# Splitting feed-forward weights into two parts once, ahead of the batch, instead of in every pass

## What is computed

```python
def _L0_ffn_ref(x, lut, gate_idx, up_idx, down_idx):      # INTER = 1376
    def _ghost_linear(x, idx, lut):
        w = lut[idx]
        return jnp.einsum('bsh,oh->bso', x, w)
    gate = _ghost_linear(x, gate_idx, lut)
    up = _ghost_linear(x, up_idx, lut)
    h = jax.nn.silu(gate) * up
    return _ghost_linear(h, down_idx, lut)
...
# the attention block: q, k, v, gates, an mLSTM mixer, h_out, then
x1 = x + h_out @ w_out
h2 = _rmsnorm(x1, norm2_w)
mlp = jax.nn.silu(h2 @ w_gate) * (h2 @ w_up) @ w_down     # FF = 2048
return x1 + mlp
...
xn = _layernorm(x, axis=-1)
x = x + _L0_attn_ref(xn, ...) + _L0_ffn_ref(xn, lut, gate_idx, up_idx, down_idx)
```

## Time and profile before

| | |
|---|---|
| median of three runs | 2799.28 us (2798.49 to 2799.92) |
| span of the profiled execution | 2801.1 us |
| look-up, from the first index load to the last predicated copy | 53 to 267 us |
| the eight passes | 267 to 2801 us |
| TensorE busy | 2441.7 us, 87% |
| VectorE, GpSimd, ScalarE busy | 1345.3, 1318.5, 1097.4 us |
| device memory read, written | 201.6 MB, 17.1 MB |
| mean granted clock of TensorE | 0.994 of full |

### The profile page before, as it was taken

One profiled execution on the slowest core, in us unless ns is written; L12 is line 12 of the kernel. 1 busy time (PEld: TensorE's weight loads), 2 busy tenths in 40 slices (PEclk: granted clock), 3 DMA queues, 4 the chain that ended last, 5 costly groups with the idle time before them and its releaser, 6 DMA issues.

```text
span 2801.1 us, 35857 instructions
## 1 busy us (share of the span) xinstructions
PE 2441.7 (87%) x11024; PEld 1970.5 (70%) x11024; DVE 1345.3 (48%) x2210; ACT 1097.4 (39%) x1847; POOL 1318.5 (47%) x887
## 2 busy tenths in 40 slices
...
GB/s 102 82 82 83 42 68 98 97 54 68 80 101 83 51 71 98 91 60 68 78 99 87 48 72 100 98 53 68 85 97 83 52 69 98 93 58 68 79 99 86
DMA packets 85664, 220.60 MB, mean 79 GB/s; under 512 B 9664, under 2 KB 9664, under 8 KB 85520
## 3 DMA queue, kind: packets, MB, share of 16 engines
...
## 4 chain that ended last, share of the span: by engine, by line
PE 42%; issue 23%; POOL 20%; DVE 8%; ACT 4%; ACTq 0%; DVEq 0%; DMA 0%; POOLq 0%; SPq 0%
PE acc L354 11%; PE gate_bank L354 10%; PE up_bank L354 10%; POOL gu_lo L1288 8%; PE bank_a L354 5%; PE bank_b L354 5%; POOL dn_lo L1293 5%; POOL hidden_lo L1298 3%; POOL MX L1313 2%; POOL vw L1328 1%; DVE hn L1088 1%; ACT acc L662 1%; DVE xn L1200 1%; DVE st L833 1%; POOL rh L1235 1%
## 5 line engine op out<-in xcount | busy, mean ns | idle before, releaser
L1298 POOL TENSOR_TENSOR hidden_lo<-hm,hidden_hi 128x512 fp32r<-128x512 f32 x216 | 279.6, 1294 | 672.4 <-ACT hidden_hi L634 672.4
L1288 POOL TENSOR_TENSOR gu_lo<-raw_gu,gu_hi 128x1024 fp32r<-128x1024 f32 x217 | 520.8, 2400 | 83.1 <-ACT gu_hi L609 83.1
L634 ACT ACTIVATE hidden_hi<-hm 128x512 fp32r<-128x512 f32 x216 | 136.3, 631 | 832.2 <-PE acc L354 813.8
L939 DVE SCALAR_TENSOR_TENSOR th<-th,gate_bank 128x512 f32<-128x512 f32 x216 | 147.7, 684 | 601.3 <-ACT th L629 601.3
L354 PE MATMUL acc<-dn_hi,hidden_hi 128*128 128x512 f32 x864 | 348.1, 403 | 10.7 <-POOL hidden_lo L1298 10.7
L354 PE MATMUL acc<-dn_hi,hidden_lo 128*128 128x512 f32 x864 | 340.8, 394 | 0.0
L354 PE MATMUL acc<-dn_lo,hidden_hi 128*128 128x512 f32 x864 | 340.6, 394 | 0.0
L1293 POOL TENSOR_TENSOR dn_lo<-raw_dn,dn_hi 128x512 fp32r<-128x512 f32 x216 | 292.3, 1353 | 63.1 <-ACT dn_hi L614 63.0
L945 DVE SCALAR_TENSOR_TENSOR hm<-th,up_bank 128x512 f32<-128x512 f32 x216 | 148.3, 687 | 251.2 <-PE up_bank L354 250.5
L629 ACT ACTIVATE th<-gate_bank 128x512 f32<-128x512 f32 x216 | 129.3, 598 | 301.9 <-PE gate_bank L354 301.9
L609 ACT ACTIVATE gu_hi<-raw_gu 128x1024 fp32r<-128x1024 f32 x217 | 226.8, 1045 | 12.5 <-DMA raw_gu<-ffn_weights 12.5
...
## 6 DMA issues: line engine op xcount, KB each, us to landing
raw_gu<-w_gu SPq DMA_DIRECT2D x128, 512.0 KB, 3.9
raw_gu<-ffn_weights SPq DMA_DIRECT2D x89, 512.0 KB, 3.7
raw_dn<-w_dn SPq DMA_DIRECT2D x128, 256.0 KB, 2.7
raw_dn<-ffn_weights SPq DMA_DIRECT2D x88, 256.0 KB, 2.7
xn<-x SPq DMA_DIRECT2D x9, 1024.0 KB, 8.4
qkT<-idx SPq DMA_DIRECT2D x34, 256.0 KB, 2.8
qkT<-x SPq DMA_DIRECT2D x8, 1024.0 KB, 5.9
result<-xn ACTq DMA_DIRECT2D x32, 256.0 KB, 2.3
```

Of the source, the lines that this page charges most:

```text
L634: act.activation(HH[0][:], hm[:], ACT.Copy).then_inc(act_hid.sem, 1)
L939: dve.scalar_tensor_tensor(th[:], th[:], 1.0, GB[:], ALU.add, ALU.mult).then_inc(vec_gate.sem, 1)
L1288: pool.tensor_tensor(WGU[1][:, slot, :], raw_gu[:, slot, :], WGU[0][:, slot, :].bitcast(f32), ALU.subtract)\
L1298: pool.tensor_tensor(HH[1][:], hm[:], HH[0][:].bitcast(f32), ALU.subtract).then_inc(pool_hid.sem, 1)
```

## The change

Device memory holds the two parts of all 27 tiles' weights, `gu_parts` and `dn_parts`, twice the bytes of the raw weights. All are written during the look-up. For the ghost chunks ScalarE casts the upper part (`upper`, between the evaluations of the chunk that follows), GpSimd subtracts, and GpSimd issues the store of both parts. For the 16 MLP tiles, which are spread over the look-up one behind every second chunk (`MLP_AFTER`), SyncE loads the raw weights, GpSimd makes both parts (`split_mlp`: two casts and two subtractions), and SyncE stores them and loads the next tile's. In the passes SyncE loads the parts into `WGU` and `WDN`, which TensorE reads (1024 KB and 512 KB a tile, two slots each); the casts and subtractions of weights on ScalarE and GpSimd are gone from there. The look-up's third chunk is built in `hr` in place of `raw_dn`.

```diff
-        ffn = nc.dram_tensor("ffn_weights", (NF, P, GU + D), f32, kind="Internal").ap()
+        gu_parts = nc.dram_tensor("gu_parts", (NT, P, 2 * GU), f32, kind="Internal").ap()
+        dn_parts = nc.dram_tensor("dn_parts", (NT, P, 2 * D), f32, kind="Internal").ap()
...
-        WGU = [sb(f"gu_{s}", [P, 2, GU], f32r) for s in ("hi", "lo")]
-        WDN = [sb(f"dn_{s}", [P, 2, D], f32r) for s in ("hi", "lo")]
+        WGU = sb("gu", [P, 2, 2, GU], f32r)
+        WDN = sb("dn", [P, 2, 2, D], f32r)
...
         BANKS = [None, A, B, GB, UB, ACC[0], ACC[1], ACC[2]]
-        wbuf = [th[:], hm[:], raw_dn[:]]
+        wbuf = [th[:], hm[:], hr[:, :, :].rearrange("p h n -> p (h n)")[:, 0:D]]
+        staged = [HT[c // 2][:, (c % 2) * 2:(c % 2) * 2 + 2, :] for c in range(3)]
+
+        def ghost_place(t, c):
+            whole, at = (gu_parts, c) if c < 2 else (dn_parts, 0)
+            return whole[t].rearrange("p (z n) -> p z n", z=2)[:, :, at * D:(at + 1) * D]
         fl = "p a b -> p (a b)"
         b0 = [qbd[:, :, :].rearrange(fl), hn[:, :, :].rearrange(fl), kn[:, 0:2, :].rearrange(fl)]
...
+        MLP_AFTER = {2 * m + 1: m for m in range(NM)}
...
-            def load_gu(at, k, slot, src):
-
-                sp.wait_ge(pool_wgu.sem, pool_wgu.of(at, k, "lo") - 2)
-                sp.dma_start(raw_gu[:, slot, :], src).then_inc(ld_gu[slot], 16)
-
-            def load_dn(at, k, src):
-                sp.wait_ge(pool_wdn.sem, pool_wdn.of(at, k, "lo") - 1)
-                sp.dma_start(raw_dn[:], src).then_inc(ld_dn, 16)
...
-            with sp.Fori(0, NF) as t:
-                for c in range(3):
-                    sp.wait_ge(look_vec, t * LOOK_V + (c * LOOK_C + LOOK_CREDIT + 3 - LOOK_V))
-                    sp.dma_start(ixb[c], idx[bass.ds(t, 1), :, c * D:(c + 1) * D].rearrange("a p n -> (a p) n"))\
-                        .then_inc(ld_idx[c], 16)
-
-            sp.wait_ge(look_vec, NF * LOOK_V + LOOK_CREDIT + 3 - LOOK_V)
-            sp.dma_start(ixb[0], idx[0, :, 0:D]).then_inc(ld_idx[0], 16)
+            def load_gu(at, k, slot, tile):
+
+                sp.wait_ge(pe_up.sem, pe_up.of(at, k, "done") - 2)
+                src = gu_parts[tile] if isinstance(tile, int) else gu_parts[bass.ds(tile, 1), :, :].rearrange("a p n -> (a p) n")
+                sp.dma_start(WGU[:, slot, :, :].rearrange("p z n -> p (z n)").bitcast(f32), src).then_inc(ld_gu[slot], 16)
+
+            def load_dn(at, k, slot, tile):
+                sp.wait_ge(pe_down.sem, pe_down.of(at, k, "done") - 2)
+                src = dn_parts[tile] if isinstance(tile, int) else dn_parts[bass.ds(tile, 1), :, :].rearrange("a p n -> (a p) n")
+                sp.dma_start(WDN[:, slot, :, :].rearrange("p z n -> p (z n)").bitcast(f32), src).then_inc(ld_dn[slot], 16)
+
+            def load_mlp(m):
+                if m >= 2:
+                    sp.wait_ge(mlp_lo, 2 * m - 3)
+                sp.dma_start(raw_gu[:, m % 2, :], w_gu[m]).then_inc(ld_mlp_gu[m % 2], 16)
+                if m >= 1:
+                    sp.wait_ge(mlp_lo, 2 * m)
+                sp.dma_start(raw_dn[:], w_dn[m]).then_inc(ld_mlp_dn, 16)
+
+            def store_mlp(m):
+                z = m % 2
+                sp.wait_ge(mlp_lo, 2 * m + 2)
+                sp.dma_start(gu_parts[NF + m], WGU[:, z, :, :].rearrange("p z n -> p (z n)").bitcast(f32)).then_inc(st_mlp[z], 16)
+                sp.dma_start(dn_parts[NF + m], WDN[:, z, :, :].rearrange("p z n -> p (z n)").bitcast(f32)).then_inc(st_mlp[z], 16)
+
+            load_mlp(0)
+            for n in range(3 * NF + 1):
+                t, c = n // 3, n % 3
+                if n >= 3:
+                    sp.wait_ge(look_vec, (t - 1) * LOOK_V + c * LOOK_C + LOOK_CREDIT + 3)
+                sp.dma_start(ixb[c], idx[t % NF, :, c * D:(c + 1) * D]).then_inc(ld_idx[c], 16)
+                if n in MLP_AFTER:
+                    m = MLP_AFTER[n]
+                    store_mlp(m)
+                    if m + 1 < NM:
+                        load_mlp(m + 1)
 
             for c in range(3):
                 sp.wait_ge(st_w[c], 16 * NF)
-            sp.wait_ge(st_zero, 16)
-            load_gu((0, 0), 0, 0, ffn[0, :, 0:GU])
+            sp.wait_ge(st_zero, 16 * 2)
+            for z in range(2):
...
                     at = (b, half)
                     for t in range(NF):
-                        nxt = ffn[t + 1, :, 0:GU] if t + 1 < NF else w_gu[0]
-                        load_gu(at, t + 1, (half * NT + t + 1) % 2, nxt)
-                        load_dn(at, t, ffn[t, :, GU:])
+                        load_gu(at, t + 1, (half * NT + t + 1) % 2, t + 1)
...
-                                    w_gu[bass.ds(i * 2 + (q + 1), 1), :, :].rearrange("a p n -> (a p) n"))
-                            load_dn(at, i * 2 + t, w_dn[bass.ds(i * 2 + q, 1), :, :].rearrange("a p n -> (a p) n"))
...
-                wait(pe, pool_wgu, at, t, "lo")
+            def parts(w, slot, n):
+                return w[:, slot, 0, n * P:(n + 1) * P], w[:, slot, 1, n * P:(n + 1) * P]
+
+            def gate(at, t, slot, act, n_loads):
+                pe.wait_ge(ld_gu[slot], n_loads)
...
+            def down(at, t, slot, n_loads, first=False, last=False):
+                pe.wait_ge(ld_dn[slot], n_loads)
                 wait(pe, pool_hid, at, t, "lo")
                 for i in range(NB):
-                    mm = split(ACC[i][:], [pair(HH, S_, toks(i))], [pair(WDN, S_, slot, S_)], first=first, last=last)
...
-
-            def w_gu(at, k, slot, n_loads):
-                act.wait_ge(ld_gu[slot], n_loads)
-                act.wait_ge(pe_up.sem, pe_up.of(at, k, "done") - 2)
-                act.activation(WGU[0][:, slot, :], raw_gu[:, slot, :], ACT.Copy).then_inc(act_wgu.sem, 1)
-
-            def w_dn(at, k, slot):
-                act.wait_ge(ld_dn, load_count_dn(at, k))
-                act.wait_ge(pe_down.sem, pe_down.of(at, k, "done") - 2)
-                act.activation(WDN[0][:, slot, :], raw_dn[:], ACT.Copy).then_inc(act_wdn.sem, 1)
...
-            def look_up(t, first=False):
+            def upper(t, c, first=False):
+
+                act.wait_ge(look_vec, t * LOOK_V + ((c + 1) * LOOK_C + LOOK_CREDIT))
+                if not first:
+                    act.wait_ge(st_w[c], t * 16)
+                act.activation(staged[c][:, 0, :], wbuf[c], ACT.Copy).then_inc(ghost_hi, 1)
...
                     act.wait_ge(look_vec, t * LOOK_V + ((c - 1) * LOOK_C + LOOK_CREDIT + 4))
                     if not first:
-                        act.wait_ge(st_w[c], t * 16)
+                        act.wait_ge(ghost_lo, (t - 1) * 3 + (c + 1))
                     for k in range(LUT // 2):
...
+                        if k == 3 and c:
+                            upper(t, c - 1, first)
+                        elif k == 3 and not first and not second:
+                            upper(t + -1, 2)
...
-            w_gu((0, 0), 0, 0, 16)
+            upper(NF - 1, 2)
+            act.wait_ge(st_zero, 16 * 2)
...
                             hid(at, t - 1)
-                        w_gu(at, t + 1, 1 - slot, gu_loads(at, t + 1))
                         tanh(at, t)
                         if t < UNITS:
...
+            def split_mlp(m):
+                z = m % 2
+                pool.wait_ge(ld_mlp_gu[z], 16 * (m // 2 + 1))
+                pool.wait_ge(st_mlp[z], 32 * (m // 2))
+                pool.tensor_copy(WGU[:, z, 0, :], raw_gu[:, z, :]).then_inc(mlp_hi, 1)
+                pool.wait_ge(ld_mlp_dn, 16 * (m + 1))
+                pool.tensor_copy(WDN[:, z, 0, :], raw_dn[:]).then_inc(mlp_hi, 1)
+                pool.wait_ge(mlp_hi, 2 * m + 2)
+                pool.tensor_tensor(WGU[:, z, 1, :], raw_gu[:, z, :], WGU[:, z, 0, :].bitcast(f32), ALU.subtract)\
+                    .then_inc(mlp_lo, 1)
+                pool.tensor_tensor(WDN[:, z, 1, :], raw_dn[:], WDN[:, z, 0, :].bitcast(f32), ALU.subtract)\
+                    .then_inc(mlp_lo, 1)
+
+            split_mlp(0)
+            for n in range(3 * NF):
+                t, c = n // 3, n % 3
+                pool.wait_ge(ghost_hi, n + 1)
+                pool.tensor_tensor(staged[c][:, 1, :], wbuf[c], staged[c][:, 0, :].bitcast(f32), ALU.subtract)\
+                    .then_inc(ghost_lo, 1)
+                pool.wait_ge(ghost_lo, n + 1)
+                pool.dma_start(ghost_place(t, c), staged[c].bitcast(f32)).then_inc(st_w[c], 16)
+                if n in MLP_AFTER and MLP_AFTER[n] + 1 < NM:
+                    split_mlp(MLP_AFTER[n] + 1)
             pool.wait_ge(vec_pre, 10)
             pool.wait_ge(st_w[2], 16 * NF)
             first = INTER - (NF - 1) * P
-            pool.dma_start(ffn[NF - 1, first:P, GU:], zero_rows[first:P, :]).then_inc(st_zero, 16)
-
-            def w_gu(at, k, slot):
-                wait(pool, act_wgu, at, k, "hi")
-                pool.tensor_tensor(WGU[1][:, slot, :], raw_gu[:, slot, :], WGU[0][:, slot, :].bitcast(f32), ALU.subtract)\
-                    .then_inc(pool_wgu.sem, 1)
...
```

(25 more changed lines are left out.)

74 lines of the change are left out of this document (26 added, 48 removed).

## The result

The changed kernel takes 2905.86 us (median of 4 runs, 2904.72 to 2906.16), the kernel before 2799.60 (4 runs, 2798.49 to 2800.13) on the same chip: 1.0381 times as long, 95% interval 1.0367 to 1.0396. The forecast was 2923, range 2855 to 3000. The profiled execution has a span of 2904.0 us, 102.9 more than before, and that splits in two: TensorE's first pass starts 174.3 us later (at 441.3 for 267.0), the passes are 73.3 us shorter together, and 1.9 are left at the program's end.

A forecast was written before the change was run, and what follows sets the result against it. TensorE was taken to bound the passes and VectorE's own chain the look-up. 2801.1 + 184 (look-up) - 2 (its end) - 58 (passes) = 2925, less 1.8 from span to median: 2923 us, range 2855 to 3000.

The forecast's parts named there:

- (d): Look-up: from the index's arrival to the end of its chunk, 5.3 us of a two-chunk period.
- (a): Look-up: ScalarE's cast, GpSimd's subtraction of 512 columns, its wait and the store's issue after a chunk, 3.1 us.
- (b): Look-up: GpSimd's split of an MLP tile, two subtractions, two casts and a semaphore, 5.65 us.
- (c): Look-up: from the tile's split to the indices' landing, behind stores and loads, 3.15 MB in all, 10.4 us.
- Part 1: The look-up: index loads held behind MLP stores in SyncE's queue start TensorE 184 us later; ScalarE's added cast costs nothing.
- the ring: Look-up: index load waits behind stores that wait for GpSimd's split after an earlier chunk; two chunks take 24.5 us, not 12.6.
- Part 2: End of the look-up: ScalarE waits for stores of zero rows, down after 8 us instead of 10; -2 us.
- Part 3: The passes: VectorE's products no longer stand still for GpSimd's subtractions, shortening TensorE's waits; 7.2 us a pass, -58 for eight.
- The rival of collisions: Look-up: GpSimd's subtractions and casts delay VectorE's bit operations up to 2.4 us a chunk, +79, total 2818; 3 in 100.
- The ring does not bind: Look-up: indices land in time, a chunk stays at 6.3 us, only the gains remain, total 2739; 4 in 100.
- The loads late: Passes: the doubled weight loads come late, 216 tiles at 1 us each, total 3138; 2 in 100.
- the gaps stay: Passes: TensorE's waits fall to the next late thing, gaining 0 to 20 us, total 2981 at most; 6 in 100.

The follow-up runs named there:

- the third run: Changed kernel with the MLP weights' split, loads and stores left out of the look-up, MLP tiles loading ghost blocks instead: 2768.19 us, 0.9884 of the kernel before.
- the first run: Changed kernel with SyncE issuing index loads ahead of the MLP transfers and storing one tile later: 2799.45 us, 0.9996 of the kernel before.
- the seventh: Changed kernel with MLP transfers behind later index loads, each split halved over two chunks, GpSimd waiting for VectorE's next bits: 2740.99 us, 0.9786 of the kernel before.

## Why the prediction was right

The cause it named decides: the index load in SyncE's queue behind the MLP transfers. Step by step, forecast and measured in one turn:

| Step | Forecast | Measured | From |
|---|---|---|---|
| (d) and (a) | 5.3 + 3.1 | 8.38 | 263.45 to 271.83 |
| (b) GpSimd's split | 5.65 | 5.27 | 271.83 to 277.10 |
| (c) to the indices | 10.4 | 10.25 | 253.19 to 263.45 |
| period | 24.5 | 23.9 (mean 24.08) | |
| TensorE's start | +184 | +174.3 | 441.3 - 267.0 |
| a pass | -7.2 | -8.55 | |
| first pass, with part 2 | -9.2 | -13.4 | |
| loads in the passes | 0 | 0 | |

The forecast was 17 us over the measured median, and 21 over the measured span: 9.7 at the start and 13.3 in the passes, less the 1.9 at the end. The 1.8 us that it took off between span and median do not carry over; the changed kernel's median is 1.9 above its profiled span.

- **Part 1.** Casts on GpSimd took 1.05 and 0.62 for the assumed 1.2 and 0.65: nearest to the memset was the right bound. The 9.7 us between 184 and 174.3 are 14 turns at 0.42 (5.9), 0.6 behind them and 3.2 at chunk 1, which ended at 76.0 for 79.2, as the first split was down at 61.0 for 63.5. The price of collisions inside the ring was put at nothing, and that held: the bits at 252.11 and 253.40 were slowed, but VectorE had to stand 8.24 us anyway, and the third, at 269.76, comes when the chunk is already with GpSimd. The slowed bits are also why VectorE stands 8.24 us and not the 12 that were forecast as a sign: a turn is 11.3 us over the 12.6 of two chunks, and 3.1 of these are the three bits. ScalarE's cast at nothing was not tested by itself; the third run, which has it, leaves at most 1.3 us for it and everything else (35.4 - 34.1).
- **The skill's figure.** By 358 GB/s (the Trainium skill, SBUF — State Buffer, summary of rules for kernel authors) (c) would by estimate be 11.0; the rows gave 10.4, and the trace has 10.25. That the rows came nearer is in part luck, for in the middle of (c), with the engines 0.99 busy, the rate is the lower one:

```profile
254.00:262.00 8.00, 0.00 (x0) 0.00 (x0) 1.21 (x2) 1.53 (x3) 1.28 (x2) 1.00 0.99 357
```

  At 357 the 3.15 MB take 8.8 us and leave 1.4 for the rest, where 2.2 was assumed: the rate was put too high, the rest too long. Another page (the Trainium skill, HBM Reference, specifications) has a core that streams alone at about 425. The 422 of the earlier trace rows agrees with that; this burst of loads and stores does not reach it.
- **Part 2** was put at -2: TensorE waits 2.5 us less for `ar` in its first pass (3.2 before, 0.7 now). Behind that wait its granted clock was 0.50 of full from 280 to 284 us, the lower of its two levels, so that twelve matmuls came every 0.43 us and not every 0.23, 2.4 us together; behind the short wait it is at full now. The forecast had counted neither, and the two make the first pass's 13.4 of the others' 8.55.
- **Part 3** was short by 1.35 a pass. Tiles 2, 4 and 6 were priced by their three waits for `tt` alone, 1.95; two tiles take 23.5 us now for 24.45, so 2.85 for the three. The remainder, 5.7, stands against 5.25 for tiles 8 and 10. The wait for `hT_lo` was to shrink by 1.0 and shrank by 0.3: L1121 (now L1144) did fall from 1.68 to 0.48, so something else ends last ahead of `hT_lo`; what it is stays open.
- **The rival of collisions** was right in mechanism and is the second cause once the ring is gone: 34 us of longer bits for the ghost subtraction alone (90.5 - 56.4), 64 with the MLP's (120.9 - 56.4); it was priced at 79. "The ring does not bind" gave 2739 with no collisions at all. In the first run, without the ring, they came in full and took the whole gain; in the seventh, without either, the time was 2741.
- **The loads late** and **the gaps stay** did not come about. Part 4 made 188 GB/s of 1.5 MB in 8.16 us; it is 193, and the trace has 192, at 0.51 of the engines for the forecast 0.6.
